# Channel normalisations by image pairs, three of them moved into the first deformable convolution

## The chip, the cores and the metric

The kernel runs on one core of one Trainium2 chip. The metric is the device time of one launch in microseconds (us); the median of three runs is 826.81 us (823.98 to 828.96).

## The reference

The input x is 8 images of 64 channels by 16 x 16 pixels, in float32. Four blocks follow, each with a residual add and each on a normalised copy of x (over the channels of every pixel):

```python
x = x + dcn_bn_relu(ln_c(x))          # 27-channel offset convolution, 9 sampled taps, batch norm, relu
t = tokens(x); t = t + lstm(ln_t(t))  # 256 steps, batch 8, hidden size 64
x = from_tokens(t); x = x + dcn(ln_c(x))
t = tokens(x); t = t + moe(ln_t(t))   # 8 experts, the best 2 of each token
# ln: (v - mean) / sqrt(var + eps)
```

## The kernel before

Partitions hold 128 channels: images 0 to 3 in the lower 64 and 4 to 7 in the upper 64, and the free axis holds four image pairs of 256 pixels, so `xs` is 128 x 1024. Each engine has its own program in program order, and semaphores join them: a wait stops everything behind it on its engine. The engines are TensorE (PE), VectorE (DVE), ScalarE (ACT) and GpSimd (POOL); SyncE (SP) issues the loads, small ones first (L340 to L355), then the expert weights.

A normalisation (`norm`, L395, L798 and L1216) goes over all 1024 columns at once: PE multiplies `xs` by a matrix of 1/64 for the means (L401), in two matmuls of 512 columns, each of two passes in float32; DVE subtracts (L1220), ACT squares (L804), PE makes variances with the squares as weights (L406, 16 passes of 2 columns), ACT takes the root (L806), DVE the reciprocal and a copy of each scale over 64 columns (L1225, L1227), PE turns them back by 8 transposes (L413), DVE multiplies (L1234). The first norm runs at the start; in its file stand also the maxima of the two sets of sampling weights (`largest`, L1333), their powers of two and the batch-norm column `bnw` (L1377 to L1387). ACT begins the convolution only when `bnw` is whole (L953). The second norm runs behind the first convolution, waits for all four residual adds (`c0_res`, L641), and takes in the recurrence's biases (`biases`, L602) while scales are made; then come the gates of row 0 (L599) and 256 recurrent steps (L658), in which PE, ACT and DVE hand over to one another and the rest of the work is laid into the gaps.

The first convolution (`conv(0)`) takes 8 images m, each in 9 steps g. On PE a step has the offsets of image m + 2 (L434, at g = 0 and 1; turned at g = 3, L443), `taps` (L456), `turn_weights(m, g)` (L469), which turns four blocks of the sampling weights `st`, and `sums` (L486), four steps behind. ACT's `high` (L870) and DVE's `low` (L1292) split each turned block into two float16 parts; `turn_weights` may be three blocks ahead of `low`, and `sums` waits for `low` too. ACT makes the tents of image m + 2 at g = 8 (L850, L854), and DVE their weighting (`weighted`, L1280), behind `low(m, 8)`. From these POOL makes `st` in six products of 768 columns for each image (`outer(m, t)`, L1143, three for each half t). After a pair is done (`turn`, L499, at g = 6 of the next even m, and ACT's `result`, L891) POOL adds it to `xs` (`add`, L1150). POOL's order is this, and the change leaves it as it is:

```python
for m, t in sorted(itertools.product(range(B), range(2)), key=lambda a: products(l, *a)):
    outer(m, t)
    if m % 2 == 0 and m > 3 and t == 0:
        add((m - 4) // 2)
for i in range(BQ - 2, BQ):
    add(i)
```

So pair 0 is added behind outer(4, 0), pair 1 behind outer(6, 0), and pairs 2 and 3 behind the last product.

## Time and profile before

| | us |
|---|---|
| median of three runs | 826.81 (823.98 to 828.96) |
| the profiled execution | 822.92 |
| its span, first to last instruction | 821.2 |
| PE busy in the span | 653.5 (80%) |
| DVE, ACT, POOL busy | 505.7, 421.4, 235.4 |

The span holds the start and first convolution (to about 136 us), the recurrence (from 146.5, at 1.58 us a step), the second convolution and the experts. Rows give the start and the busy time in us, the engine, the line, the operation, what it writes and reads with its shape, and a count where instructions of one kind are merged. In brackets stands how long the engine stood idle before, and what ended that. PE's matmuls are pipelined and their ends modelled. PEclk is TensorE's granted clock, 1.00 for 2.4 GHz.

### The profile page before, as it was taken

The page shows a single profiled execution, that of the slowest core. Times are in us where ns is not written, and L with a number is a line of the kernel's source. Part 1 is how long each engine was busy: PE and PEld are TensorE (multiplying, and loading weights), DVE is VectorE, ACT ScalarE, POOL GpSimd, SP SyncE. Part 2 cuts the span into 40 slices and gives each one's busy share as a digit, 9 for nine tenths or more (in the row PEclk, how much of TensorE's full clock was granted, in tenths as well). Part 3 has the DMA queues.
Part 4 walks back from the last instruction along what each step waited for, and adds up shares of the span by engine and source line. Part 5 has one row for each costly group of instructions (what it writes and reads, how often), then busy time and mean ns, then how long its engine had stood idle before and what let it go on. Part 6 is the DMA issues. An engine that isn't in the chain of part 4 may idle for free.

```text
span 821.2 us, 16043 instructions
## 1 busy us (share of the span) xinstructions
PE 653.5 (80%) x5315; PEld 524.9 (64%) x5315; DVE 505.7 (62%) x1672; ACT 421.4 (51%) x1492; POOL 235.4 (29%) x209
## 2 busy tenths in 40 slices
PE   5799998666787667776689888976899961999991
PEld 3478787555566555655566656654788961788881
DVE  4688884456654566655434444344888878688883
ACT  3476775233333555553334444446677771677760
POOL 0587682000000000000002100000887601677751
PEclk9999999555555555555555555555899985899996
DMA  9910000000000000000000000000000000111112
GB/s 211 212 32 2 2 2 1 2 1 0 1 2 1 1 1 1 2 0 1 1 0 2 1 1 2 1 1 1 1 2 2 2 2 29 23 28 27 28 21 81
DMA packets 12769, 14.97 MB, mean 18 GB/s; under 512 B 5873, under 2 KB 8626, under 8 KB 12690
## 3 DMA queue, kind: packets, MB, share of 16 engines
q1 hardware_dynamic: 9906, 11.26, 6.1%
q0 software_dynamic: 2496, 2.56, 1.5%
q8 instruction: 45, 0.74, 0.4%
q14 instruction: 34, 0.28, 0.1%
q10 hardware_dynamic: 288, 0.13, 0.1%
HBM read 11.62 MB, written 2.33 MB: 17 GB/s over the span
## 4 chain that ended last, share of the span: by engine, by line
PE 58%; DVE 17%; ACT 13%; issue 8%; DMA 2%; DVEq 1%; SPq 1%; POOL 0%; POOLq 0%; ACTq 0%
PE bank L486 7%; DVE bank L1510 6%; PE duo L736 6%; PE duo L664 6%; PE bank L664 5%; DVE hr L1514 4%; PE bank L469 4%; ACT duo L1036 4%; PE duo L434 4%; ACT bank L1040 4%; PE duo L666 3%; PE bank L666 3%; PE bank L747 3%; PE bank L762 3%; PE duo L469 3%
## 5 line engine op out<-in xcount | busy, mean ns | idle before, releaser
L1143 POOL TENSOR_TENSOR st<-tent,tentx 128x768 f32<-128x768 f32 x72 | 112.5, 1592 | 172.9 <-DVE tentx L1284 123.5
L1510 DVE TENSOR_TENSOR_SCAN bank<-duo,scan_add 64x24 f32<-64x24 f32 x256 | 52.8, 206 | 125.4 <-ACT duo L1036 125.1
L1143 POOL TENSOR_TENSOR st<-sq 128x768 f32<-128x768 f32 x9 | 13.2, 1500 | 305.7 <-DVE sq L1499 305.7
L668 PE MATMUL bank<-hr,lv 64*64 64x8 f32 x512 | 91.5, 251 | 0.0
L664 PE MATMUL bank<-hr,lv 64*64 64x8 f32 x256 | 48.5, 261 | 51.5 <-DVE hr L1514 51.4
L664 PEld LDWEIGHTS bank<-hr,lv 64*64 64x64 f32 x256 | 36.3, 201 | 81.2 <-DVE hr L1514 81.1
L664 PE MATMUL duo<-hr,lv 64*64 64x8 f32 x256 | 48.5, 261 | 46.5 <-DVE hr L1514 46.2
L664 PEld LDWEIGHTS duo<-hr,lv 64*64 64x64 f32 x256 | 36.3, 201 | 76.3 <-DVE hr L1514 76.0
L1514 DVE SCALAR_TENSOR_TENSOR hr<-tog,bank 64x8 f32<-64x8 f32 x256 | 39.6, 155 | 73.4 <-ACT bank L1040 73.4
L668 PEld LDWEIGHTS bank<-hr,lv 64*64 64x64 f32 x512 | 84.4, 223 | 0.0
L486 PE MATMUL bank<-zw,shi 128*128 128x128 f16 x576 | 79.6, 220 | 1.1 <-ACT osb L880 0.8
L486 PE MATMUL bank<-zw,hid 128*128 128x128 f16 x576 | 79.6, 220 | 0.0
L1292 DVE SCALAR_TENSOR_TENSOR hid<-bank,shi 128x512 f16<-128x512 f32 x96 | 64.7, 686 | 18.5 <-ACT shi L870 17.9
L1036 ACT ACTIVATE duo<-duo 64x16 f32<-64x16 f32 x128 | 19.6, 153 | 102.1 <-PE duo L666 101.9
L870 ACT ACTIVATE shi<-bank 128x512 f16<-128x512 f32 x96 | 57.2, 596 | 28.2 <-PE bank L469 27.3
L1036 ACT ACTIVATE duo<-bank 64x16 f32<-64x16 f32 x128 | 19.6, 153 | 93.6 <-PE bank L666 93.4
L469 PE MATMUL bank<-ident,st 128*128 128x128 f32 x384 | 60.5, 282 | 1.6 <-DVE hid L1292 1.4
L486 PEld LDWEIGHTS bank<-zw,shi 128*128 128x128 f16 x576 | 56.7, 99 | 2.2 <-DVE hid L1292 1.9
L486 PEld LDWEIGHTS bank<-zw,hid 128*128 128x128 f16 x576 | 56.7, 98 | 1.6
L736 PE MATMUL duo<-w13s,st 128*128 x312 | 54.1, 318 | 1.3 <-ACT st L1087 1.3
L1040 ACT ACTIVATE bank<-bank 64x8 f32<-64x8 f32 x256 | 37.6, 147 | 29.7 <-DVE bank L1510 2.2
L1038 ACT ACTIVATE tog<-bank 64x8 f32<-64x8 f32 x256 | 43.8, 171 | 15.2
(257 smaller groups left out, 1564.4 us busy)
## 6 DMA issues: line engine op xcount, KB each, us to landing
w13s<-w SPq DMA_DIRECT2D x16, 320.0 KB
w2s<-w SPq DMA_DIRECT2D x4, 320.0 KB
st<-yrows SPq DMA_DIRECT2D x2, 512.0 KB, 4.6
st<-xrows,xidx POOLq DMA_INDIRECT x39, 2.5
yrows<-st,yidx POOLq DMA_INDIRECT x39, 2.2
samw<-sample_w SPq DMA_DIRECT2D x2, 288.0 KB, 4.2
xs<-x SPq DMA_DIRECT2D x2, 256.0 KB, 4.2
xrows<-st SPq DMA_DIRECT2D x1, 512.0 KB, 2.6
```

Of the source, the lines that this page charges most:

```text
L469: mm = nc.tensor.transpose(bank[3 + g % RING][:, k * 128:k * 128 + 128], st[m % 2][:, t, tap, half * 128:half * 128 + 128], ident[:, :])
L486: mm = nc.tensor.matmul(bank[6][:, lo:lo + 2 * C], part[:, place(p, h), k, :], zw[p][:, half, tap, :, :].rearrange("p k c -> p (k c)"), st ...
L664: nc.tensor.matmul(both[:, 0, t, :], lv[:, C:2 * C], prev, start=False, stop=True, skip_group_check=True)
L668: nc.tensor.matmul(go, lv[:, 2 * C:3 * C], prev, start=False, stop=True, skip_group_check=True).then_inc(s("l_o"), 1)
L736: mm = nc.tensor.matmul(duo[m][:, half * 512:half * 512 + n], xts[:, t % 3, :], w16[:, bass.ds(e * SLOT + at, n)], start=(part == 0), stop ...
L870: nc.scalar.activation(shi[:, place(m % 2, g), :, :].rearrange("p k n -> p (k n)"), bank[3 + g % RING][:, :], ACT.Copy, scale=SSCALE / (1 ...
L1036: nc.scalar.activation(gate_in[:, 1:3, :], both, ACT.Tanh).then_inc(s("l_act"), 1)
L1040: nc.scalar.activation(tcell[:, :], cell[:, :, 2], ACT.Tanh, scale=0.5).then_inc(s("l_tc"), 1)
L1143: nc.gpsimd.tensor_tensor(st[p][:, t, k:k + KG, :].rearrange("p k (y x) -> p k y x", x=16), ty, tx, ALU.mult)\
L1292: nc.vector.scalar_tensor_tensor(out=slo[:, place(m % 2, g), :, :].rearrange("p k n -> p (k n)"), in0=bank[3 + g % RING][:, :], scalar=SSC ...
L1510: nc.vector.tensor_tensor_scan(cell[:, :, :].rearrange("p b k -> p (b k)"), gates, scan_add[:, :, :].rearrange("p b k -> p (b k)"), 0.0, A ...
L1514: nc.vector.scalar_tensor_tensor(out=hr[:, n % (2 * W), :], in0=tog[:, :], scalar=1.0, in1=tcell[:, :], op0=ALU.add, op1=ALU.mult).then_in ...
```

## The change

- SP loads the second set of sampling weights (`samw[1]`) fifth, and the second offset weights (`convw[1]`) later, under another semaphore.
- Both normalisations go by pairs of 256 columns, with helpers on each engine. At the start pair 0 is done through to its scaled columns first, and the roots, scales and scaling of the other three come inside the convolution's first images. ACT's wait for `bnw` stands behind `pads(2)`.
- Of the second normalisation, pair i = 0, 1, 2 is centred, squared and its variance taken inside the convolution, at m = 3, 5 and 7: PE's mean at g = 1 (behind a wait for that pair's add), DVE's centring at g = 2, ACT's square at g = 3, PE's variance at g = 5, and DVE's copy of it into `dev` at g = 6. Mean and variance lie in free or finished columns of bank 7. Pair 3 is done behind the convolution, and one root takes the three kept pairs.
- The scales of the recurrence's input are turned and applied in two halves of the rows: the first half ahead of step 0 (row 0 first), the second in steps 0 to 3.

```diff
             sp.dma_start(convb[:, :], conv_b).then_inc(s("ld_conv"), 16)
             sp.dma_start(samw[0][:, :], sample_w[0]).then_inc(s("ld_conv"), 16)
             sp.dma_start(bnp[:, :], bn).then_inc(s("ld_conv"), 16)
+            sp.dma_start(samw[1][:, :], sample_w[1]).then_inc(s("ld_conv"), 16)
             sp.dma_start(rank_c[:, :], consts[:, 2 * P:2 * P + E]).then_inc(s("ld_const"), 16)
             sp.dma_start(tent_c[:, :, :, :, :].rearrange("p a b c d -> p (a b c d)"),
                          consts[:, 2 * P + E:]).then_inc(s("ld_const"), 16)
-            sp.dma_start(convw[1][:, :, :, :], conv_w[1]).then_inc(s("ld_conv"), 16)
-            sp.dma_start(samw[1][:, :], sample_w[1]).then_inc(s("ld_late"), 16)
+            sp.dma_start(convw[1][:, :, :, :], conv_w[1]).then_inc(s("ld_late"), 16)
...
-            def norm(l, ready, middle=None, end=None):
...
+            def mean_of(i, to):
+
+                nc.tensor.matmul(to, mean_w[:, :], pixels(xs, 0, P, i), start=True, stop=True)\
+                    .then_inc(s("n_mean"), 1)
+
+            def variance_of(l, i, to, start):
+
+                pe.wait_ge(s("n_sq"), BQ * l + i + 1)
                 for j in range(2):
+                    mm = nc.tensor.matmul(to[:, 2 * j:2 * j + 2], sq[:, i * T + j * 128:i * T + j * 128 + 128],
+                                          mean_w[:, 0:P:C], start=(start and j == 0), stop=True,
+                                          skip_group_check=True)
+                return mm
...
+            def turn_scales(i):
+
+                for j in range(2):
+                    mm = nc.tensor.transpose(bank[(0, 5, 6, 7)[i]][:, T + j * 128:T + j * 128 + 128],
+                                             sq[:, i * T + j * 128:i * T + j * 128 + 128], ident[:, :])
+                mm.then_inc(s("n_rt"), 1)
+
+            def turn_row_scales(q):
+
+                pe.wait_ge(s("n_rb"), 3 + q)
+                for i in range(BQ):
+                    mm = nc.tensor.transpose(bank[2 - q][:, i * 128:i * 128 + 128],
+                                             sq[:, i * T + q * 128:i * T + q * 128 + 128], ident[:, :])
+                mm.then_inc(s("n_rt"), 1)
 
...
+                        if l == 0:
+                            pe.wait_ge(s("n_keep"), i)
...
                 offsets(0, 0)
                 offsets(0, 1)
+                if l == 0:
+                    pe.wait_ge(s("n_rb"), 2)
+                    turn_scales(1)
                 turn_offsets(0)
                 pe.wait_ge(s(c + "taps"), 2)
                 taps(0, 0)
+                if l == 0:
+                    turn_scales(2)
+                    turn_scales(3)
                 offsets(1, 0)
                 offsets(1, 1)
                 turn_offsets(1)
                 taps(0, 1)
+                if l == 0:
+                    pe.wait_ge(s("n_xn"), BQ)
                 for m in range(B):
                     for g in range(NG):
+                        if l == 0 and m > 2 and m % 2 == 1:
+                            if g == 1:
+                                pe.wait_ge(s("c0_res"), m // 2)
+                                mean_of(m // 2 - 1, bank[7][:, T:2 * T])
+                            elif g == 5:
+                                variance_of(1, m // 2 - 1, bank[7][:, 0:4], True).then_inc(s("n_var"), 1)
                         if m + 2 < B:
                             if g < 2:
                                 offsets(m + 2, g)
...
-            norm(0, [("ld_x", 32)], turn_max, spread)
+            pe.wait_ge(s("ld_x"), 32)
+            mean_of(0, bank[0][:, 0:T])
+            mean_of(1, bank[5][:, 0:T])
+            variance_of(0, 0, bank[4][:, 0:4], True).then_inc(s("n_var"), 1)
+            mean_of(2, bank[6][:, 0:T])
+            mean_of(3, bank[7][:, 0:T])
+            pe.wait_ge(s("n_rb"), 1)
+            turn_scales(0)
+            variance_of(0, 1, bank[4][:, 4:8], False)
+            variance_of(0, 2, bank[4][:, 8:12], False)
+            turn_max()
+            variance_of(0, 3, bank[4][:, 12:16], False).then_inc(s("n_var"), 1)
+            spread()
             pe.wait_ge(s("ld_conv"), 16 * 5)
-            pe.wait_ge(s("n_xn"), 2)
             conv(0)
...
-            norm(1, [("c0_res", BQ)], biases)
-            pe.wait_ge(s("n_xn"), 4)
+            pe.wait_ge(s("c0_res"), BQ)
+            mean_of(3, bank[1][:, 0:T])
+            variance_of(1, 3, bank[2][:, 0:4], True).then_inc(s("n_var"), 1)
+            biases()
+            turn_row_scales(0)
+            pe.wait_ge(s("n_xn"), 5)
...
-                if n == POWER + 2:
+                if n == 1:
+                    turn_row_scales(1)
+                    pe.wait_ge(s("n_xn"), 6)
+                elif n == POWER + 2:
...
+                    if n == 7 * W + SLOTS[0]:
+                        pe.wait_ge(s("n_xn"), 8)
                     gates_x(r + 1, SLOTS.index(t))
...
+            def square_of(l, i):
+
+                act.wait_ge(s("n_xc"), BQ * l + i + 1)
+                nc.scalar.activation(pixels(sq, 0, P, i), pixels(xc, 0, P, i), ACT.Square).then_inc(s("n_sq"), 1)
+
+            def root_of(src, lo, hi, eps):
+
+                nc.scalar.activation(dev[:, lo:hi], src, ACT.Sqrt, bias=epsc[:, eps:eps + 1]).then_inc(s("n_sd"), 1)
...
+                    if l == 0:
+                        act.wait_ge(s("n_xn"), b4 + 1)
...
+                if l == 0:
+                    act.wait_ge(s("n_var"), 2)
+                    root_of(bank[4][:, 4:16], 4, 16, 0)
+                    act.wait_ge(s("ld_conv"), 16 * 5)
+                    nc.scalar.activation(bnw[:, 0:1], bnp[:, 3:4], ACT.Sqrt, bias=epsc[:, 1:2]).then_inc(s("bn_a"), 1)
+                    nc.scalar.preload_act_table(ACT.Sigmoid)
                 offsets(0)
...
+                if l == 0:
+                    act.wait_ge(s("bn_d"), 6)
+                    act.wait_ge(s("c_scale"), 2)
...
+                        if l == 0 and m > 2 and m % 2 == 1 and g == 3:
+                            square_of(1, m // 2 - 1)
...
-            norm(0, 0, ACT.Sqrt)
-            act.wait_ge(s("ld_conv"), 16 * 5)
-            nc.scalar.activation(bnw[:, 0:1], bnp[:, 3:4], ACT.Sqrt, bias=epsc[:, 1:2]).then_inc(s("bn_a"), 1)
-            nc.scalar.preload_act_table(ACT.Sigmoid)
-            act.wait_ge(s("bn_d"), 6)
-            act.wait_ge(s("c_scale"), 2)
+            nc.scalar.preload_act_table(ACT.Sqrt)
+            square_of(0, 0)
+            square_of(0, 1)
+            act.wait_ge(s("n_var"), 1)
+            root_of(bank[4][:, 0:4], 0, 4, 0)
+            square_of(0, 2)
+            square_of(0, 3)
             conv(0)
 
 
-            norm(1, 1, ACT.Tanh)
+            nc.scalar.preload_act_table(ACT.Sqrt)
+            act.wait_ge(s("n_keep"), 3)
+            root_of(dev[:, 0:12], 0, 12, 1)
+            square_of(1, 3)
+            act.wait_ge(s("n_var"), 6)
+            root_of(bank[2][:, 0:4], 12, 16, 1)
+            nc.scalar.preload_act_table(ACT.Tanh)
             def high_part(k):
...
+            def centre_of(l, i, src):
+
+                dve.wait_ge(s("n_mean"), BQ * l + i + 1)
+                nc.vector.tensor_tensor(pixels(xc, 0, P, i), pixels(xs, 0, P, i), src, ALU.subtract)\
+                    .then_inc(s("n_xc"), 1)
+
+            def scales_of(lo, hi):
+
+                dve.wait_ge(s("n_sd"), 1 if lo == 0 else 2)
+                nc.vector.reciprocal(dev[:, lo:hi], dev[:, lo:hi]).then_inc(s("n_rs"), 1)
+                dve.wait_ge(s("n_rs"), 1 if lo == 0 else 2)
+                nc.vector.tensor_copy(sq[:, lo * C:hi * C].rearrange("p (k c) -> p k c", c=C),
+                                      dev[:, lo:hi].unsqueeze(2).broadcast_to([P, hi - lo, C])).then_inc(s("n_rb"), 1)
+
+            def scaled(i):
+
+                dve.wait_ge(s("n_rt"), i + 1)
+                nc.vector.tensor_tensor(pixels(xn, 0, P, i), pixels(xc, 0, P, i), bank[(0, 5, 6, 7)[i]][:, T:2 * T],
+                                        ALU.mult).then_inc(s("n_xn"), 1)
+
+            def row_scales(q):
+
+                nc.vector.tensor_copy(half_rows(sq[:, :], q).rearrange("p b (k c) -> p b k c", c=C),
+                                      half_rows(dev[:, :], q).unsqueeze(3).broadcast_to([P, BQ, 2, C]))\
+                    .then_inc(s("n_rb"), 1)
+
+            def scaled_rows(q, lo, hi):
+
+                dve.wait_ge(s("n_rt"), BQ + q + 1)
+                nc.vector.tensor_tensor(half_rows(xn[:, :], q)[:, :, lo:hi], half_rows(xc[:, :], q)[:, :, lo:hi],
+                                        bank[2 - q].rearrange("p (b n) -> p b n", b=BQ)[:, :, lo:hi],
+                                        ALU.mult).then_inc(s("n_xn"), 1)
...
-                    dve.wait_ge(s("n_xn"), 2)
                     flats(0)
-                    split_taps(l)
+                    normalised()
...
                 distances(0)
+                if l == 0:
+                    scaled(1)
                 weighted(0)
                 tap_images(0, 0)
+                if l == 0:
+                    scaled(2)
+                    scaled(3)
                 distances(1)
                 flats(1)
...
+                        if l == 0 and m > 2 and m % 2 == 1:
+                            if g == 2:
+                                centre_of(1, m // 2 - 1, bank[7][:, T:2 * T])
+                            elif g == 6:
+                                i = m // 2 - 1
+                                dve.wait_ge(s("n_var"), 3 + i)
+                                nc.vector.tensor_copy(dev[:, 4 * i:4 * i + 4], bank[7][:, 0:4])\
+                                    .then_inc(s("n_keep"), 1)
                         if g == 3 and m + 2 < B:
...
-            def largest():
+            def largest(l):
 
                 dve.wait_ge(s("ld_conv"), 80)
-                dve.wait_ge(s("ld_late"), 32)
-                for l in range(2):
-                    nc.vector.tensor_reduce(cmax[:, l:l + 1], samw[l][:, :], AX.X,
-                                            ALU.max, apply_absolute_value=True).then_inc(s("c_max"), 1)
+                nc.vector.tensor_reduce(cmax[:, l:l + 1], samw[l][:, :], AX.X,
+                                        ALU.max, apply_absolute_value=True).then_inc(s("c_max"), 1)
 
...
+            def normalised():
+
+                scales_of(4, 16)
+                split_taps(0)
+                dve.wait_ge(s("bn_a"), 1)
+                nc.vector.reciprocal(bnw[:, 1:2], bnw[:, 0:1]).then_inc(s("bn_d"), 1)
...
+            centre_of(0, 0, bank[0][:, 0:T])
+            centre_of(0, 1, bank[5][:, 0:T])
+            scales_of(0, 4)
+            centre_of(0, 2, bank[6][:, 0:T])
+            largest(0)
+            centre_of(0, 3, bank[7][:, 0:T])
+            scaled(0)
+            largest(1)
+            power("c", cpow, bank[3], KTOP)
+            dve.wait_ge(s("c_bc"), 1)
+            nc.vector.reciprocal(csc[:, :, 0], bank[3][:, 256:258]).then_inc(s("c_scale"), 1)
+            nc.vector.tensor_scalar(csc[:, :, 1], bank[3][:, 256:258], 2.0 ** (KTOP - ZTOP) / SSCALE, None,
+                                    ALU.mult).then_inc(s("c_scale"), 1)
             conv(0)
-            norm(1)
-            dve.wait_ge(s("n_xn"), 3)
+            centre_of(1, 3, bank[1][:, 0:T])
             nc.vector.memset(gates, 0.0).then_inc(s("l_zero"), 1)
+            dve.wait_ge(s("n_sd"), 4)
+            nc.vector.reciprocal(dev[:, :], dev[:, :]).then_inc(s("n_rs"), 1)
+            dve.wait_ge(s("n_rs"), 3)
+            row_scales(0)
+            scaled_rows(0, 0, W)
+            scaled_rows(0, W, 128)
 
...
+                if n == 0:
+                    row_scales(1)
+                elif 2 <= n <= 3:
+                    scaled_rows(1, 64 * (n - 2), 64 * (n - 1))
```

## Rows read from the trace of the kernel before

**Rows 1.** Table of stretches, the convolution; us, busy us (instructions) by engine, PEclk, DMA

```profile
core 0: us, PE busy (x) PEld busy (x) DVE busy (x) ACT busy (x) POOL busy (x), PEclk, DMA share, GB/s
40.00:130.00 90.00, 87.73 (x948) 73.27 (x947) 77.22 (x118) 64.31 (x143) 66.38 (x45) 1.00 0.05 12
```

**Rows 2.** Timeline of the start, all engines

```profile
6.19 3.75 PE L401 MATMUL duo<-xs,mean_w 128*128 128x512 f32 x4 [6.19 <-DMA xs<-x]
...
9.74 3.51 PE L406 MATMUL duo<-mean_w,sq 128*128 128x2 f32 x16
...
12.60 1.41 DVE L1338 TENSOR_REDUCE cmax<-samw 128x1 f32<-128x576 f32 x2 [1.92 <-DMA rw<-router]
...
16.85 0.58 PE L561 MATMUL duo<-cpow,ones 1*128 1x2 f32 x2
...
18.61 1.70 ACT L823 COPY pad<-xn 64x256 f32<-64x256 f32 x4 [2.13 <-DVE bnw L1387]
...
19.59 5.25 PE L434 MATMUL duo<-pad,convw 128*27 128x256 f32 x12 [2.16 <-ACT pad L823]
...
26.23 2.77 PE L434 MATMUL duo<-pad,convw 128*27 128x256 f32 x12
```

**Rows 3.** Chain that ended last, from the last add to the recurrence; start, us, what

```profile
135.55 0.73 POOL xs L1150
136.33 1.14 PE duo L401 x2
...
138.89 1.95 PE duo L406 x16
140.84 1.04 PE duo L594 x4
...
142.31 1.91 PE duo L413 x8
...
144.99 1.11 PE duo L599 x8
...
146.53 0.31 PE duo L664 x2
```

**Rows 4.** Timeline of PE, one recurrent step

```profile
149.68 0.38 PE L664 MATMUL duo<-hr,lv 64*64 64x8 f32 x2 [0.78 <-DVE hr L1514]
```

**Rows 5.** Timeline of ACT, a table load and the instruction behind it

```profile
13.58 1.28 ACT L808 ACT_TABLE_LOAD   x1
...
14.88 0.29 ACT L951 ACTIVATE bnw<-bnp,epsc 128x1 f32<-128x1 f32 x1
```

**Rows 6.** Timelines of DVE, POOL and PE in the convolution, around the adds

```profile
74.22 0.45 DVE L1280 TENSOR_TENSOR tentx<-tent,sig 128x288 f32<-128x288 f32 x1
...
74.84 4.63 POOL L1143 TENSOR_TENSOR st<-tent,tentx 128x768 f32<-128x768 f32 x3 [4.72 <-PE duo L469]
79.44 0.72 POOL L1150 TENSOR_TENSOR xs<-xs,ores 128x256 f32<-128x256 f32 x1
...
106.42 0.72 POOL L1150 TENSOR_TENSOR xs<-xs,ores 128x256 f32<-128x256 f32 x1
...
123.05 0.73 POOL L1150 TENSOR_TENSOR xs<-xs,ores 128x256 f32<-128x256 f32 x1
...
75.10 1.48 PE L434 MATMUL duo<-pad,convw 128*27 128x256 f32 x6
...
123.91 0.60 PE L469 MATMUL bank<-ident,st 128*128 128x128 f32 x4
```

**Rows 7.** Table of stretches and PE's timeline, where its clock moved; columns as in rows 1

```profile
133.00:136.00 3.00, 1.16 (x8) 0.97 (x8) 0.00 (x0) 1.72 (x4) 0.45 (x1) 1.00 0.00 0
...
670.00:671.00 1.00, 0.26 (x3) 0.16 (x2) 0.93 (x3) 0.01 (x1) 0.00 (x0) 1.00 0.00 0
...
673.00:674.00 1.00, 0.00 (x0) 0.00 (x0) 0.90 (x5) 0.99 (x3) 0.00 (x0) 0.60 0.00 0
...
567.58 2.73 PE L434 MATMUL duo<-pad,convw 128*27 128x128 f32 x12 [2.08 <-ACT pad L823]
...
570.00:571.00 1.00, 0.55 (x4) 0.20 (x3) 0.00 (x0) 0.36 (x1) 0.00 (x0) 0.60 0.00 0
```

More of the change, by code:

```diff
@@ L262, in build, with half_rows @@
             s(n)
-        def nth(l):
-            return min(l, 2)
+        def half_rows(t, q):
+            return t.rearrange("p (b q n) -> p b q n", b=BQ, q=2)[:, :, q, :]
         def pixels(t, p0, p1, b4):
@@ L394, in _ @@
         def _(pe):
-            def norm(l, ready, middle=None, end=None):
-                for wait_sem, v in ready:
-                    pe.wait_ge(s(wait_sem), v)
-                for j in range(2):
-                    nc.tensor.matmul(bank[j][:, :], mean_w[:, :], xs[:, j * 512:j * 512 + 512],
-                                     start=True, stop=True).then_inc(s("n_mean"), 1)
-                for j in range(8):
-                    if j % 4 == 0:
-                        pe.wait_ge(s("n_sq"), 2 * nth(l) + j // 4 + 1)
-                    mm = nc.tensor.matmul(bank[2][:, 2 * j:2 * j + 2], sq[:, j * 128:j * 128 + 128],
-                                          mean_w[:, 0:P:C], start=(j == 0), stop=True, skip_group_check=True)
-                mm.then_inc(s("n_var"), 1)
-                if middle:
-                    middle()
-                pe.wait_ge(s("n_rb"), nth(l) + 1)
-                for j in range(8):
-                    mm = nc.tensor.transpose(bank[j // 4][:, j % 4 * 128:j % 4 * 128 + 128],
-                                             sq[:, j * 128:j * 128 + 128], ident[:, :])
-                    if j % 4 == 3:
-                        mm.then_inc(s("n_rt"), 1)
-                if end:
-                    end()
```

71 lines of the change are left out of this document (17 added, 54 removed).

## The prediction

> **What bounds the kernel now.** I read the table of stretches first, then the timeline and the chain of waits at three places: the start, the seam between first convolution and recurrence, and the third and fourth image of the convolution. In the convolution [rows 1] the reader is to see that TensorE (PE) is busy 87.73 of 90 us, with VectorE at 77.22, ScalarE at 64.31 and GpSimd (POOL) at 66.38: time added to PE there, or a wait of PE, is paid almost in full, since the other engines catch up while it stands. The unused rest, 2.27 us of 90, is some 0.3 us for an image of about 13 us. Ahead of it stands a serial start [rows 2]: x lands, the first mean matmul goes at 6.19, and the first offset convolution only at 19.59. Behind it stands a serial seam [rows 3]: the last add on POOL at 135.55, the whole normalisation after it, the recurrence's first matmul at 146.53. The change works on both seams and puts the difference into the PE-bound part.
>
> **Start.** Before, DVE waits for the last small load before it takes the two maxima (12.60, 1.41 us), and ScalarE's pads wait for the batch-norm column until 18.61 [rows 2]. Afterwards the first pair's pads wait for its own scaled columns alone, and what ends last is PE's queue. Its order, at the pace of those rows: two means of 256 columns, half of the 3.75 us of L401, so ready at 7.4 and 8.3; DVE's centring and ScalarE's square of pair 0 to 8.35; its variance, a quarter of the 3.51 us of L406, to about 9.3; two means, 1.75, to 11.05; two transposes, a quarter of the 1.91 us of the seam's L413 [rows 3], to 11.55; two variances to 13.4; the maxima's transposes, taken at the 0.58 us of L561, to 14.0; the fourth variance to 14.95; the spread matmul, 0.58, to 15.55. So the offsets start near 15.6 instead of 19.59: 4.0 us early. samw1 is now fifth in the queue and convw1 goes behind; the first is needed at 12.3 and was complete at 12.60 even as a late load, so nothing waits for either. Of the rest, turn_scales(1) hides behind ScalarE's bias copy of the offsets, the other two pairs' transposes (4, at full pace about 0.5 us) come ahead of the second image's offsets on PE, and DVE's three scalings fall into idle time ahead of the next distances. Net: **-3.5**. Bounds: -2 if PE takes a second longer to come to full pace, which it did while the 12 passes of 19.59 ran (5.25 us, against 2.77 at 26.23), -5 if that happens sooner.
>
> **Seam.** Only pair 3 is left there. From 136.33 [rows 3]: the mean of 256 columns instead of 512, about 0.7 instead of 1.14; centring and square, 1.42 us from the end of the mean to 138.89, go to about 0.95; 4 variance passes instead of 16, 0.5 instead of 1.95; the biases, 1.47 us between 140.84 and 142.31, stay and hide root, reciprocal and the copy of half the scales; four transposes instead of eight, 0.96 instead of 1.91; one scaling of 64 columns, about 0.3 instead of the 0.77 between 144.22 and 144.99; the gates' 1.54 stay. That ends at 142.75: **-3.8**, between -3 (half pace already at the mean) and -4.5. The other row half costs its four transposes behind the step n = 1: 0.96 us against 0.78 us of PE idle in a step [rows 4], **+0.2**, at most +1; DVE's copies and scalings of n = 0 to 3 stand in steps whose weight maxima start only at n = 4, and hide.
> A table load is where a rule can be weighed: ScalarE's next instruction starts at 14.88, 0.02 us after a load of 1.28 us from 13.58 [rows 5]. So the square-root table, loaded while POOL adds, is there in time, and the sum above holds. The Trainium skill (ScalarE: Activation LUTs, What ACT_TABLE_LOAD costs) adds a drain and gives about 2.66 us for a switch; by that the square of pair 3 would wait some 0.6 us and the seam bring -3.2 as an estimate from that page. The trace disagrees with it by the 0.02 us.
>
> **Inside the convolution, work.** At m = 3, 5 and 7 PE gets a mean (2 passes of 256 columns, 0.23 each by the 2.77 us for 12 at 26.23 [rows 2]) and a variance (4 passes at 0.12 by 138.89 [rows 3]): 0.96 us, three times **+2.9**. DVE gets a centring of 256 columns and a copy of 4, ScalarE a square, some 1.4 us together at each place. They stand in one file (low g = 2, centring, square, high g = 3), so they delay DVE's chain by about 0.95 us; PE itself is later by more than that at that point, so I take nothing, and keep 0 to +1 for each of m = 3 and 5.
>
> **Inside the convolution, the new wait.** This is the step that decides. PE takes mean_of(0) at m = 3, g = 1, behind a wait for c0_res 1, and that is POOL's add(0). POOL's order is not changed: add(0) stands behind outer(4, 0), which needs weighted(4), and DVE makes that at m = 2, g = 8. The rows [rows 6] show the three in a line: DVE's tentx at 74.22, POOL's three products from 74.84, the add at 79.44 for 0.72, so xs is ready at 80.16. PE is at that place (ahead of offsets(5, 1)) at 75.10. It would stand 80.2 - 75.1 = 5.1 us. Queued behind it on PE are the second half of the offsets, all turn_weights of the image and the sums, so ScalarE's highs and DVE's lows run dry as well; nothing else feeds PE. The same pattern comes once more, at m = 5 (the add at 106.42 [rows 6]). At m = 7 the add is at 123.05 and done at 123.77, PE is there at 123.91: no wait. Nothing in the change brings the add forward, since start and image 2 shift all engines alike. Two waits, less the 0.3 us of slack each: **+9.6**. Bounds: +8 (POOL at its best pace and more slack found), +11 (m = 7 late as well).
> **The clock after such a gap.** PE fell idle in 670 to 671, and within 673 to 674, whose mean is 0.60, its granted clock fell from 1.00 to 0.50, the 1.2 GHz level: some 3 us after the last matmul [rows 7]. A gap of 5.1 us is longer than that, so I expect the fall at both places. After dense work began at 567.58 the clock rose within 570 to 571, 3 us later [rows 7]; at the start it took 5.25 us at half pace [rows 2]. Of 3 to 5.3 us at half pace half is lost: 1.5 to 2.6, I take 2.1, twice **+4.2**; without a fall 0.
> The Trainium skill (TensorE: Matmul & The Clock Gate, Why this matters for your kernels) warns of idle gaps between matmul bursts as what throws the clock back to its half rate. By that rule each of the two waits costs more than its own length; the trace agrees, in the fall at 673.
>
> **Sum.** -3.5 - 3.8 + 0.2 + 2.9 + 9.6 + 4.2 = **+9.6 us**. The profiled execution took 822.92 us, its span and 1.7 us around it; with the sum, 832.5. The median of the runs shown is 826.81, 3.9 above it, and the sum does not hang on that difference: 826.81 + 9.6 = **836.4 us**, 1.2% slower. About 0.5% (4.1 us) is what a measurement of this kernel can tell from no change.
>
> **The rivals.** (a) The clock holds through the gaps. For it: PE had only 1.16 us of matmul between 133 and 136 and the granted clock stayed at 1.00 [rows 7]. Against: that was broken by bursts, this gap is not. Then +5.4: 832.2, slower by 0.65%. (b) The wait costs nothing, faster. Its mechanism is that add(0) is done before PE gets to g = 1 of m = 3, because PE is held back in image 2 or POOL gets weighted(4) earlier. It decides if the add ends 5.1 us earlier against PE. Price: no waits, no clock loss, -4.2: 822.6, 0.5% faster. Against it stands the row itself: the products before the add alone take 4.6 us, and they start with the data of the last step of the image before. (c) The waits come, but their gap is filled: DVE and ScalarE are ahead when PE resumes and some of the 2.27 us idle and the start's early clock bring more than I gave; start -5, seam -4.5, the step +0.2, work +2.9, waits +8, no fall: +1.6, 828.4, no difference. (d) Dearer: DVE's chain adds 1 us at m = 3 and 5 and the clock takes 5.3 us to return: 9.6 + 2 + 1.1 = +12.7, 839.5.
>
> **How the numbers follow.** My forecast with its bounds, 0.58; (d) 0.08; (a) 0.18; (c) 0.08; (b) 0.08. The likeliest is the forecast. The range 830.5 to 840.5 holds it with its bounds taken one at a time, (d) and most of (a), about 0.8, and leaves out (b) and (c). Slower by over 0.5%: 0.58 + 0.08 + 0.18 less 0.04 for the low end of (a), 0.80; within 0.5%: that 0.04, (c), and some 0.02 of (b), 0.14; faster 0.06.
>
> **What would show it.** In the changed profile: the first L434 row near 15.6; the recurrence's first matmul some 6.5 us after the end of the last add, where it was 10.2; PE idle before mean_of(0) and mean_of(1) for about 5 us each, released by POOL's xs, and none before mean_of(2); PE's granted clock at 0.50 for 3 to 5 us behind both. The prediction is wrong if PE has no such two gaps, or if the first offsets and the recurrence do not move.

## The result and the profile after

The changed kernel takes 840.34 us (median of six runs, 838.25 to 841.30), the kernel before 827.67 beside it (823.98 to 828.96): ratio 1.0169, 95% interval 1.0143 to 1.0194, slower. The direction was right. The ratio is just past the high end of the range (840.5 / 826.81 = 1.0166); the two medians differ by 12.7 us, where 9.6 was forecast, and 840.34 itself lies just inside, so the interval covers the end of the range. The profiled execution took 838.25 us with a span of 836.5, where before it was 822.92 and 821.2: 15.3 us more in the two spans, 12.7 in the medians.

First PE's waits from 20 to 165 us, longest first; the columns are the total in us, the times, and the longest one.

```profile
PE bank L397 <- POOL xs L1205: 10.0, 2, 5.0
PE duo L438 <- issue: 4.0, 1, 4.0
```

The first line is new, and it is the predicted wait: PE's mean (L397) stands twice for 5.0 us until POOL has added the pair (L1205). The timelines of POOL and PE at both places, and then at the third mean, show the three in a file:

```profile
78.45 0.72 POOL L1205 TENSOR_TENSOR xs<-xs,ores 128x256 f32<-128x256 f32 x1
...
79.22 1.22 PE L397 MATMUL bank<-xs,mean_w 128*128 128x256 f32 x2 [5.02 <-POOL xs L1205]
...
113.46 0.72 POOL L1205 TENSOR_TENSOR xs<-xs,ores 128x256 f32<-128x256 f32 x1
...
114.23 1.22 PE L397 MATMUL bank<-xs,mean_w 128*128 128x256 f32 x2 [5.02 <-POOL xs L1205]
...
138.95 0.65 PE L397 MATMUL bank<-xs,mean_w 128*128 128x256 f32 x2
```

The third mean, at 138.95, has no such bracket. Next, the table of stretches (columns as in [rows 1]) around the first of these gaps and behind the second:

```profile
75.00:77.80 2.80, 0.00 (x0) 0.00 (x0) 2.08 (x3) 0.00 (x0) 2.80 (x3) 0.97 0.00 0
77.80:84.60 6.80, 5.38 (x19) 2.83 (x20) 0.00 (x0) 0.39 (x1) 5.71 (x5) 0.51 0.00 0
84.60:111.00 26.40, 24.32 (x259) 20.02 (x255) 20.04 (x36) 18.95 (x44) 11.62 (x8) 1.00 0.01 2
111.90:118.80 6.90, 4.57 (x12) 2.07 (x13) 0.25 (x1) 0.00 (x0) 6.62 (x5) 0.51 0.00 0
```

PE does nothing from 75.0 to 77.8, and in the next 6.8 us its granted clock is at half, the 1.2 GHz level: that is why the mean takes 1.22 us. The convolution before never left 1.00 [rows 1].

The start, from its timeline (all engines):

```profile
15.66 4.72 PE L438 MATMUL duo<-pad,convw 128*27 128x256 f32 x12
...
24.52 12.64 POOL L1198 TENSOR_TENSOR st<-tent,tentx 128x768 f32<-128x768 f32 x8 [22.92 <-DVE tentx L1349]
...
26.11 1.96 DVE L1339 TENSOR_TENSOR dist<-tent_c,omt 128x576 f32<-128x576 f32 x1 [0.36 <-ACT omt L876]
...
29.50 0.82 ACT L862 COPY pad<-xn 64x256 f32<-64x256 f32 x2
...
30.41 2.73 PE L438 MATMUL duo<-pad,convw 128*27 128x256 f32 x6 [3.99 <-issue]
```

The same place in the kernel before (VectorE's distances of the second image, PE's offsets of the third):

```profile
30.13 0.88 DVE L1270 TENSOR_TENSOR dist<-tent_c,omt 128x576 f32<-128x576 f32 x1 [0.65 <-ACT omt L837]
...
33.32 1.48 PE L434 MATMUL duo<-pad,convw 128*27 128x256 f32 x6 [2.86 <-ACT pad L823]
```

The offsets start at 15.66 for 19.59 [rows 2], as predicted. The third image's offsets do not keep that: PE stands 3.99 us before them, for 2.86, and runs them at half pace (2.73 us; 1.48 before).

And the seam, from the chain that ended last (start, us, what), to be held against [rows 3]:

```profile
151.69 0.73 POOL xs L1205
152.42 0.04 issue
152.46 0.98 PE duo L397 x2
...
154.39 1.02 PE duo L404 x4
155.41 1.04 PE duo L625 x4
...
156.87 1.06 PE duo L420 x4
...
158.23 1.11 PE duo L630 x8
...
159.77 0.31 PE duo L699 x2
```

From the end of the last add to the first recurrent matmul it is 7.35 us, where it was 10.25 [rows 3].

With these lines the whole difference can be laid out. The table gives, for each profiled execution, the start of VectorE's first low part (L1292 before, L1361 after), the time from the first low part of image m to that of the next, image 7 to its last low part, from the start of the last add to the last multiply of step 0 (L1514, L1607), the 255 further steps, and what is left of the span. The missing columns, m = 2, 4, 6 and the way from the last low part to the last add, are 13.85, 13.85, 9.47 and 4.14 us everywhere (in e10 to e12 m = 4 is 14.24).

```
                 first   m=0    m=1    m=3    m=5   m=7   seam   steps    rest
before           36.05  12.98  12.51  13.14  12.45  7.11  12.34  413.11  260.2
after            34.56  12.61  13.41  21.16  20.43  8.22   9.45  415.37  260.0
e1_add_first     34.35  13.70  13.41  13.90  13.58  8.21   8.79  415.38  262.6
e2_waits_only    37.65  12.31  12.46  19.93  19.85  7.11  13.74  413.03  260.0
e3_filled        35.07  12.32  13.40  18.71  18.38  8.25   8.93  415.40  262.5
e4_start_only    34.50  12.58  13.41  13.14  12.45  7.11  13.75  413.52  261.3
e5_pads_early    32.87  13.49  12.46  13.90  13.57  8.22   9.70  415.32  262.7
e8_before_shift5 36.81  13.19  13.40  13.14  12.45  7.11  12.32  412.71  261.5
e9_start_pads    32.23  13.27  12.46  13.14  12.45  7.11  12.33  413.01  261.6
e10_late         34.01  13.69  13.41  13.14  13.00  8.22   9.70  415.22  262.7
e12              32.38  13.49  12.46  13.14  12.99  8.22   9.39  412.17  260.1
```

After less before: -1.5, -0.4, +0.9, **+8.0, +8.0**, +1.1, -2.9, +2.3, -0.2, in all +15.3.

Each row is one execution, and some columns move with the moment at which the granted clock falls. The old seam took 12.3 us where the clock fell 5 to 6 us behind the start of the last add (before, e8, e9), and 13.75 where it fell 0.3 and 1.2 us behind it (e2, e4), with the same code.

### The profile page after: what moved, and what is told of

Its sections match the earlier page's. It is cut to its first block, busy times and chain, and to the rows that moved or that the text cites. A ratio compares the mean times of both kernels' runs of the same rounds, so it can differ in the third digit from the quotient of the medians.

```text
span 836.5 us, 16090 instructions
## 1 busy us (share of the span) xinstructions
PE 659.6 (79%) x5323; PEld 529.0 (63%) x5323; DVE 504.1 (60%) x1686; ACT 420.8 (50%) x1497; POOL 234.3 (28%) x209
## 4 chain that ended last, share of the span: by engine, by line
PE 57%; DVE 16%; ACT 13%; issue 10%; DMA 2%; POOL 1%; DVEq 1%; SPq 0%; POOLq 0%; ACTq 0%
PE bank L490 6%; PE duo L776 6%; DVE bank L1603 6%; PE duo L699 6%; PE bank L699 5%; DVE hr L1607 4%; PE bank L473 4%; ACT duo L1091 4%; ACT bank L1095 4%; PE duo L438 4%; PE duo L701 3%; PE bank L701 3%; PE bank L787 3%; PE bank L802 3%; PE duo L473 2%
## 5 line engine op out<-in xcount | busy, mean ns | idle before, releaser
L1361 DVE SCALAR_TENSOR_TENSOR hid<-bank,shi 128x512 f16<-128x512 f32 x96 | 65.0, 686 | 34.6 <-ACT shi L909 33.7
L1607 DVE SCALAR_TENSOR_TENSOR hr<-tog,bank 64x8 f32<-64x8 f32 x256 | 39.7, 155 | 74.6 <-ACT bank L1095 74.6
```

The costliest lines, as they stand in the source:

```text
L1361: nc.vector.scalar_tensor_tensor(out=slo[:, place(m % 2, g), :, :].rearrange("p k n -> p (k n)"), in0=bank[3 + g % RING][:, :], scalar=SSC ...
L1607: nc.vector.scalar_tensor_tensor(out=hr[:, n % (2 * W), :], in0=tog[:, :], scalar=1.0, in1=tcell[:, :], op0=ALU.add, op1=ALU.mult).then_in ...
```

## The experiments

The theory was that the two waits, with the half clock behind them, make the slowdown. The rivals: the added work in the PE-bound convolution; a start or seam that failed; and, for the recurrence's +2.3, something in the program's layout.

**e1: the add goes first.** GpSimd is idle before the product that the add stood behind.

```diff
+                    if l == 0 and m % 2 == 0 and m > 3 and t == 0:
+                        add((m - 4) // 2)
                     outer(m, t)
-                    if m % 2 == 0 and m > 3 and t == 0:
+                    if l == 1 and m % 2 == 0 and m > 3 and t == 0:
                         add((m - 4) // 2)
```

> The changed kernel, but GpSimd runs the add of image pairs 0 and 1 ahead of the product of the even image that it stood behind (in the first convolution only). ores of pair 0 is ready at 70.3 us and GpSimd is idle from 68.9 to 73.9, so the add ends near 71.1, before TensorE comes to the mean at 74.2. Theory (the two waits on the add and the half clock behind them make the slowdown): both 5.0 us gaps of TensorE go, and no half clock near 78 and 112; step m=3 and step m=5 fall back from 15.1 and 16.5 us to about 13.2 and 14.6 (12.1 and 13.5 before, and 1.1 of added work, as step m=7 shows). That is 4 us less in all than the waits and the clock: 14 less 0.2, so 838.25 - 13.8 = 824.5 for the profiled execution and 840.3 - 13.8 = 826.5 for the median, against 827.7 before: ratio 0.996 to 1.001. Rival (the added instructions on TensorE, VectorE and ScalarE, and the stir they make in the convolution, cost the time, and the wait only shows where it is lost): at most half of it goes, 833 or more, ratio over 1.006.

Measured: 825.73 us (twelve runs) against 825.36, ratio 0.9999 (0.9981 to 1.0016). The timelines of POOL and PE:

```profile
71.23 0.73 POOL L1205 TENSOR_TENSOR xs<-xs,ores 128x256 f32<-128x256 f32 x1 [1.45 <-ACT ores L930]
...
74.92 0.65 PE L397 MATMUL bank<-xs,mean_w 128*128 128x256 f32 x2
```

The add is done 3 us before PE asks, nothing stands, and the granted clock is 1.00 from 75 to 120. Moving one line takes back the whole 1.7%. Steps m = 3 and 5 keep 0.8 and 1.1 us over the kernel before: that is the work.

**e2: the waits alone**, in the kernel before.

```diff
                     for g in range(NG):
+                        if l == 0 and m in (3, 5) and g == 1:
+                            pe.wait_ge(s("c0_res"), m // 2)
```

> The kernel before, with nothing but two waits added: TensorE waits for the add of pair 0 at m=3, g=1 and for that of pair 1 at m=5, g=1; no work is added or moved. Theory: TensorE is the bound there, so each wait costs its whole length (it comes at 75.1 and 102.2 where the adds end at 80.2 and 107.2 or later, 5 us each) and the half clock behind it 2 us more: 827.7 + 14 = 841.7, ratio 1.017, TensorE idle 5 us at L434 before each and a granted clock of 0.50 for some 7 us from about 3.5 us into each gap. Rival (other engines' slack takes the waits up, and the added work is what costs): 828 to 832, ratio under 1.006.

Measured: 839.11 us, ratio 1.0163 (1.0135 to 1.0191). PE's waits from 60 to 120 us, and the stretches behind the two gaps:

```profile
PE duo L434 <- POOL xs L1152: 10.0, 2, 5.0
```

```profile
79.70:86.50 6.80, 5.43 (x27) 3.52 (x28) 0.69 (x1) 1.00 (x3) 5.65 (x5) 0.53 0.01 2
...
113.80:120.60 6.80, 5.75 (x30) 3.77 (x30) 0.69 (x1) 1.14 (x3) 5.33 (x5) 0.53 0.00 0
```

Two waits with no work behind them cost what the whole change costs (6.8 and 7.4 us in the table). With e1 it settles the cause from both sides. The trace also bears on the start, whose code is that of the kernel before:

```profile
33.17 2.76 PE L434 MATMUL duo<-pad,convw 128*27 128x256 f32 x6 [2.86 <-ACT pad L825]
...
31.50:38.30 6.80, 5.13 (x14) 2.19 (x15) 4.75 (x7) 2.16 (x5) 6.80 (x5) 0.50 1.10 207
```

Behind the same gap of 2.86 us, after which PE ran at full pace in the kernel before, the granted clock is at half here; in e8 it also fell, at 34.2.

**e3: the gap filled.** Ten matmuls, whose results are overwritten, ahead of each of the two waits (and behind a wait for their output columns to be free), in the changed kernel.

```diff
                             if g == 1:
+                                pe.wait_ge(s("c0_out_sb"), m // 2)
+                                for _ in range(10 if m < 7 else 0):
+                                    nc.tensor.matmul(bank[7][:, T:2 * T], mean_w[:, :], pixels(xs, 0, P, 3),
+                                                     start=True, stop=True)
                                 pe.wait_ge(s("c0_res"), m // 2)
```

> The changed kernel, and ahead of the two waits TensorE multiplies ten times the mean matrix by 256 columns of pair 3 into the half bank that the mean takes next (about 0.49 us each, 4.9 us: what the wait lasts), so that it stands still no longer; the results are overwritten. Theory of the clock: the wait ends when it did, but no half clock follows at 78 and 112, the mean takes 0.49 us again for 1.22, the offsets behind it 1.41 for 2.69, steps m=3 and m=5 13.1 for 15.1 and 14.5 for 16.5: 838.25 - 4 = 834.2 for the profiled execution, 836.3 for the median. Rival (the half clock costs nothing, since other engines have slack enough, or the dummy work delays the rest): 840 or more.

Measured: 835.48 us, ratio 1.0118 (1.0092 to 1.0144). PE's timeline at m = 3, and the stretch around it:

```profile
74.26 4.54 PE L544 MATMUL bank<-xs,mean_w 128*128 128x256 f32 x20
79.46 0.70 PE L397 MATMUL bank<-xs,mean_w 128*128 128x256 f32 x2 [0.67 <-POOL xs L1209]
80.09 1.48 PE L438 MATMUL duo<-pad,convw 128*27 128x256 f32 x6
```

```profile
75.00:90.00 15.00, 14.34 (x132) 12.01 (x131) 8.27 (x15) 6.64 (x16) 8.76 (x7) 1.00 0.00 0
```

The wait ends when it did, the clock stays at 1.00, and the offsets take 1.48 us again. So each 8.0 us divides: for m = 3 (m = 5) the half clock is 21.16 - 18.71 = 2.45 (2.05), the wait 18.71 - 13.90 = 4.81 (4.80), the work 13.90 - 13.14 = 0.76 (1.13).

**e4: the start alone.** The second normalisation goes back whole behind the convolution (the code of the kernel before, with the changed semaphore counts).

> The changed kernel's start alone: the first normalisation by image pairs; all four pairs of the second behind the convolution, as before. Theory: the start's gain is real but TensorE's longer gap before the third image's offsets (4.0 us for 2.9) and the half clock behind it take most of it: step m=3 is reached 0.9 us earlier than before and the seam lasts 10.2 us: 822.9 - 0.9 = 822.0 for the profiled execution, 826.8 for the median, ratio 0.998 to 1.000. Rival (the start gives its full 3.5 us, lost later by what was put into the convolution): 824.2, ratio 0.996. Second rival (the 2 us that the changed kernel lost inside the recurrence come from the program's new layout at the start): 828.8.

Measured: 824.28 us against 825.36, ratio 0.9986 (0.9970 to 1.0002). The 2 us in the recurrence do not come with the start (413.52). By the traces the start brings 1.0 us over the kernel before: 1.5 at the first low part and 0.4 in m = 0, less 0.9 in m = 1. The median alone does not exclude the full 3.5 us: in e4's trace the old seam took 1.4 us more than in the kernel before, which hides part of a gain.

**e5: what ate the start's gain.** On top of e1, ScalarE pads the third image ahead of the second's tents, in the time in which it waits for VectorE's distances anyway.

```diff
                 taps(0, 1)
+                if l == 0:
+                    pads(2)
                 tents(1)
-                pads(2)
+                if l == 1:
+                    pads(2)
```

> e1_add_first, and ScalarE copies the third image's padded input (pads(2)) ahead of the tents of the second image instead of behind them, in the first convolution. ScalarE is idle from 26.96 to 28.10 there, waiting for VectorE's distances, and the copies take 0.82, so nothing else moves. Theory (the start's gain is lost because TensorE stands 4.0 us before the third image's offsets, where it stood 2.9, and the clock falls behind that): the gap falls to 1.0 to 1.6 us, no half clock between 29 and 36, the first low part comes 2 to 3 us earlier than in e1_add_first and the step from the first to the second image takes 12.3 to 12.6 us for 13.7: 2.5 to 4 us less than e1_add_first, ratio to before 0.995 to 0.997. Rival (GpSimd's products of images 0 and 1, 9.5 us each from 24.5 on, or VectorE's time beside them, set the pace there): under 1.2 us less, ratio 0.998 to 1.001.

Measured: 820.79 us against 825.27, ratio 0.9942 (0.9923 to 0.9961), more than expected. The timeline:

```profile
26.18 1.96 DVE L1344 TENSOR_TENSOR dist<-tent_c,omt 128x576 f32<-128x576 f32 x1 [0.35 <-ACT omt L876]
...
26.92 0.83 ACT L862 COPY pad<-xn 64x256 f32<-64x256 f32 x2
27.85 1.46 PE L438 MATMUL duo<-pad,convw 128*27 128x256 f32 x6 [1.34 <-issue]
```

PE's gap falls from 3.99 to 1.34 us, the offsets run at full pace, the first low part comes at 32.87 and m = 1 takes 12.46. A half clock still comes, later (from 37.3 to 40.8, behind a gap of 2.13 us), within m = 0, which takes 13.49. (The profiled execution took 825.28 us, 4.5 more than the median, so its table row understates the gain.)

**e6 and e8: the recurrence's 2 us.** In the kernel before, four of the 255 steps take 1.93 us for 1.58 with nothing in the way, in the changed kernel eight others. Step 22 of the kernel before on VectorE, and the ScalarE row that it waits for:

```profile
181.10 0.15 DVE L1514 SCALAR_TENSOR_TENSOR hr<-tog,bank 64x8 f32<-64x8 f32 x1 [0.28 <-ACT bank L1040]
...
182.19 0.21 DVE L1510 TENSOR_TENSOR_SCAN bank<-duo,scan_add 64x24 f32<-64x24 f32 x1 [0.43 <-ACT duo L1036]
183.03 0.15 DVE L1514 SCALAR_TENSOR_TENSOR hr<-tog,bank 64x8 f32<-64x8 f32 x1 [0.64 <-ACT bank L1040]
...
182.43 0.15 ACT L1040 ACTIVATE bank<-bank 64x8 f32<-64x8 f32 x1
```

ScalarE is done at 182.58; the multiply starts 0.45 us later, 0.1 in a usual step. Both experiments move VectorE's later instructions by a few places (three in e6, on top of e1; five in e8, in the kernel before):

```diff
+            for k in range(3):
+                nc.vector.memset(csc[:, 0, k % 2:k % 2 + 1] if k < 2 else csc[:, 1, k % 2:k % 2 + 1] if k < 4 else cmax[:, 0:1], 0.0)
             nc.vector.memset(ones[:, :], 1.0).then_inc(s("l_init"), 1)
```

> e1_add_first, and three more memsets of one column at the very start of VectorE's program, where it waits for xs until 6.7 us; nothing else. It tests where the changed kernel's 2 us inside the recurrence come from: steps of 1.93 us for 1.58 in which VectorE starts the last multiply of the step 0.35 us late with everything it waits for done. Counted in VectorE's instructions, these multiplies stand at places 62 of 64 (19, 38, 114, 133, 153 by 64, and two later places), in the kernels before, after and of the start alone. Theory (VectorE stands 0.35 us at every 64th instruction of its program, and the change has moved the step's last multiply onto such places more often): three instructions more move all of 19, 38, 114, 133, 153, 175 and 196 off, one (142) comes on; the 255 steps take 413.2 us for 415.4, 2.1 us less than e1_add_first. Rival (the steps are slow by time or by what runs beside them): the same steps stay slow, 415.4.

Measured: 414.03 us for the steps (1.35 less; 2.1 expected), median 824.11, ratio 0.9977 (0.9956 to 0.9998). All seven named steps became quick; 142 did not become slow, and 76, 95, 195 and 216 did.

> The kernel before, with five one-column memsets at the start of VectorE's program and nothing else. By the same count no last multiply of a step stands at place 62 of 64 any more: the steps 22, 79, 136 and 199 (1.93 us) go back to 1.58 and 145 (2.16) to 1.8 or less; the 255 steps take 411.3 to 411.8 us for 413.1, the median 1.3 to 1.8 us less, ratio 0.998 to 0.9985. Rival (the slow steps don't hang on VectorE's place in its program): 413.1, the same steps slow, ratio 1.000.

Measured: 412.71 us for the steps (0.40 less), median 825.72, ratio 0.9998 (0.9979 to 1.0017): no gain in the median. All four named steps became quick, 145 stayed, 177 became slow. So the slow steps do hang on the place in VectorE's program, and the rival falls; but the count by 64 missed some. Laid over six traces, a count by 128 fits without exception: a step's last multiply at place 62 or 64 of 128 is late, at 59 to 61, 63 and 65 to 67 it is not (step 2 is slow by the second row half, put into step 1; why 200 is slow is not known). The count takes in the waits of VectorE's program; over the trace's own records, from 0, the places are 63 and 65. Both are one place: where the multiply stands at 64, it is the scan of its step, two places ahead, that is late. Step 175 of the changed kernel shows it, a scan 0.46 us behind the end of the ScalarE row that it waits for (442.16):

```profile
442.62 0.21 DVE L1603 TENSOR_TENSOR_SCAN bank<-duo,scan_add 64x24 f32<-64x24 f32 x1 [0.60 <-ACT duo L1091]
```

In all 14 traces, each of the 51 multiplies and 20 scans at place 62 started about 0.35 us later behind its wait than is usual, and no multiply at another place did. e12 puts the count to the test.

**e7: e5 and e6 together.**

> e5_pads_early and e6_shift3 together. Theory: the two add up, 4.5 to 6 us less than e1_add_first, ratio to before 0.992 to 0.995. Rival: the pace elsewhere takes them up, 0.996 or more.

Measured: 821.85 us, ratio 0.9955 (0.9935 to 0.9974), 3.9 us under e1 and not under e5. The steps took 414.05 us, as in e6; the medians do not add up (e5 gained 4.9 us on e1, e6 1.6), which their intervals of 1.6 us to either side allow, and the expectation of 4.5 to 6 was too high.

**e9: is the part inside the convolution worth anything?** e4 with the early pads of e5.

> e4_start_only with the pads of the third image early as in e5: the whole second normalisation stays behind the convolution. It asks whether the part inside the convolution is worth anything once its waits are gone. Theory (a wash: 0.8 + 1.1 + 1.1 us of added TensorE time per pair, against some 3.5 us less at the seam and 2 us more of slow steps in the recurrence): 819.5 to 821.5, within 0.2% of e5's 820.8, ratio to before 0.992 to 0.996. Rival (the seam's part is worth its 3.5 us): 823 to 825, ratio 0.997 to 0.999.

Measured: 821.12 us, ratio 0.9943 (0.9922 to 0.9965), the same as e5. By the traces the part inside the convolution gains 2.6 us at the seam (9.70 for 12.33), and pays 3.0 in m = 3, 5 and 7 and 2.3 in the steps; the medians, 820.79 and 821.12, show no difference.

**e10: PE asks later.** GpSimd's order stays; for pairs 0 and 1 the mean moves from g = 1 to g = 6, and the centring, square and variance behind it move as well (not shown).

```diff
-                        if l == 0 and m > 2 and m % 2 == 1:
-                            if g == 1:
+                        if l == 0 and (m, g) in ((3, 6), (5, 6), (7, 1)):
```

> The changed kernel with GpSimd's order left as it is, and TensorE's mean of pairs 0 and 1 moved from g=1 to g=6 of images 3 and 5, the steps behind it with it (centre at g=7, square at g=8, the variance and the copy of it at g=1 and g=2 of the next image); pair 2 stays. TensorE comes to the mean near 82 and 110 us, the adds end at 79.2 and 107. Theory (what costs is where TensorE waits, not the work): no wait on the add in images 3 and 5, no half clock there, the same as e1_add_first, 825 to 827, ratio to before 0.998 to 1.002. Rival (the add's place behind GpSimd's product hurts in itself, as ores then comes free late for the next pair): 830 or more.

Measured: 824.28 us against 826.45, ratio 0.9972 (0.9956 to 0.9989). POOL's and PE's timelines:

```profile
79.01 0.72 POOL L1205 TENSOR_TENSOR xs<-xs,ores 128x256 f32<-128x256 f32 x1
...
81.44 0.65 PE L397 MATMUL bank<-xs,mean_w 128*128 128x256 f32 x2
```

The add's place does not hurt in itself. The work costs less here, too: 0.0, 0.4 and 0.55 us in m = 3, 4 and 5, for 0.76 and 1.13 in e1.

**e11 and e12: everything together.** e11 is e10 with the early pads; e12 adds four memsets on VectorE, the number for which no step's multiply stands at place 62 or 64 of 128.

> e10_late and the early pads of e5 together: the whole change with both repairs. Theory: the two don't touch, so 824.3 less the 3 to 4.5 us that the early pads gave in e5 and e9: 820 to 821.5, ratio to before 0.991 to 0.995, no better than e5 and e9 beyond 0.2%. Rival (the late mean spares the work inside the convolution too, since step m=3 of e10 lasted 13.14 us as before): 817 to 819, ratio 0.988 to 0.991.

Measured: 821.93 us, ratio 0.9946 (0.9926 to 0.9965): the ratio as the theory had it, the time 0.4 us above its 820 to 821.5.

> e11_late_pads and four one-column memsets at the start of VectorE's program. The runs so far corrected the count of e6 and e8: in the traces of before, after, e4, e6, e8 and e10 every recurrent step whose last multiply stands at place 62 or 64 of 128 of VectorE's program is 0.35 us late, and no other place near it (steps 2 and 200, slow for another reason, aside). That explains the misses of e6 (142 stayed quick, 76 and 95 came) and e8 (145 stayed, 177 came). With four more instructions no step's multiply stands at such a place. Theory: the eight slow steps of e11 (19, 38, 114, 133, 153, 175, 196, 237) all go and none comes, the 255 steps take 412.3 us for 415.1; the median falls by 2.8 us to 819.1, ratio to before 0.990 to 0.993. Rival (the places were fitted to the runs by chance): three to eight slow steps stand somewhere, 413.4 or more.

Measured: none of the eight slow steps is left and none has come; the 255 steps take 412.17 us (412.3 expected). The median is 818.63 us (six runs) against 825.05, ratio 0.9929 (0.9904 to 0.9954). This version is faster than both kernels, by 0.7% than the one before: the whole change, with the means of two pairs moved, one copy moved and four empty instructions. e9 with such a shift was not run, so it is not shown that the part inside the convolution adds to that.

## Why the prediction was right and wrong

- **The waits: right, to 0.1 us.** +9.6 was the term, 4.81 + 4.80 was measured; the third mean had no wait. Rival (b), the add done before PE asks, fell at the row it was argued from, and e1 shows what it would have been worth.
- **The clock behind them: right.** +4.2 predicted, 2.45 + 2.05 measured, with a fall 3.5 and 2.6 us into the gaps. The half clock lasted 6.8 us, longer than the 3 to 5 I gave, but part of it lay over the rest of the gap, where PE had nothing to run. Rival (a) fell.
- **The work: right.** +2.9 predicted, 0.76 + 1.13 + 1.11 = 3.0 measured. In e10 it cost 0.0 + 0.4 + 0.55 + 1.1, a third less, so the place matters as well.
- **The start: the step that failed most.** -3.5 was the term, -1.0 the measurement. The first 4 us came as worked out. But the step took the gain at the first offsets for that of the whole start ("start and image 2 shift all engines alike"), and that was wrong: GpSimd's first product came 4.4 us earlier and VectorE's distances of the second image 4.0, and beside each other these distances now took 1.96 us for 0.88. ScalarE's pads stand behind them, so PE's gap before the third image grew from 2.86 to 3.99 us: 1.1 of the 4 us. Another 1.3 went as the clock fell behind that gap (offsets of 2.73 us for 1.48). That the growth of the gap brought the fall is not shown: behind the old gap of 2.86 us the clock fell in e2 and e8 as well, and held in the one profiled execution of the kernel before. Up to the end of m = 1 the changed kernel is 1.0 us ahead of that execution, 1.8 ahead of e2 and 2.8 ahead of e8, so part of this miss is luck, in the clock and in how VectorE and GpSimd fall together. I had priced the start by its first offsets and not by the next thing that PE waits for. e5 cut the gap to 1.34 us and gained 4.9 us on e1.
- **The seam: mechanism right, term too large.** -3.8 was the term, -2.9 the measurement. The clock fell 1.1 us behind the start of the last add, at 152.8, before 5.2 us behind it, at 140.7, so mean and variance ran at half pace (0.98 and 1.02 us in the chain, for 0.7 and 0.5 in the sum), which is 0.8 of the missing 0.9; -3 was the bound for that case. Where it fell 3.0 us behind the add (e1) the seam took 8.79 us, -3.55; at 1.1 us (after) 9.45, at 0.5 us (e5, e10) 9.70. The step that failed here took the clock's fall from where the old seam had it, and that moves too: against the old seam with an early fall (13.75 us, e4) the new one gains 4.3.
- **The recurrence: not foreseen.** +0.2 was the term, for step 1, and +2.3 the measurement. Step 1 to 2 does cost 0.2. Of the other 2.1 us, 1.4 are slow steps that new instructions on VectorE, far ahead of them, moved onto bad places (e6, e8, e12): eight of 0.35 us for four. Step 200 is another 0.3; the rest is not accounted for.
- In all, the terms that decided the sign (waits, clock, work) were right to 0.5 us. What failed are the net of the start (2.5 us too large), the seam (0.9) and the recurrence (2.1 us put at nothing): 5.5 of the 5.7 us between the forecast and the two spans. That rival (d) came to the 12.7 us of the medians is luck; its terms, a longer VectorE chain and a longer half clock, are not what was measured. What stays open: the last part of the span took 260.0 to 264.1 us from one profiled execution to another, in kernels that differ little there. The traces place 2.6 us of it at the start of the second convolution: from the recurrence's last multiply to the seventh low part, 24.9 us in the kernel before, where the granted clock first rose 9.8 us behind that multiply, and 27.5 in e1, where it stayed at half for 26 us. Why it rose so differently is not known, and it is one reason why sums of one trace and medians differ by a few us. Nor was the new order of the loads tried by itself.

## What to carry to other kernels

Before a wait is put on the engine that bounds a stage, compare two rows: when the engine gets there, and when the awaited instruction ends, with all that is queued ahead of it on its own engine. If the second is later, here nearly every microsecond was paid, and almost half as much again as the clock fell; the cure is often to move one line, on either side. A gain at the start of a pipeline is worth what the next wait of the bounding engine leaves of it, so follow it to the next gap.

## What the hardware showed that was not expected

- **VectorE stands about 0.35 us at one place in every 128 of its program**, and it shows where a dependent chain has no slack: a step of 1.58 us becomes 1.93. In 14 traces, all 71 multiplies and scans of the recurrence at that place were late, and the forecast of e12 rested on it. Four empty instructions were worth 3.0 us of the recurrence (415.13 to 412.17). The Trainium skill (Runtime: NRT & Kernel Launch, Instruction fetch mechanics) has instructions fetched in blocks of 256, mostly hidden; that these stalls are such a fetch is not shown here, and the period that the runs show is 128.
- **VectorE's distances took from 0.76 to 1.96 us**: 0.76 at 25.98 in the kernel before, with GpSimd idle, up to 1.96 beside GpSimd's products of 1.58 each on average, by how the two fall together. With the five memsets of e8 m = 1 took 13.40 us for 12.51, and its distances 1.58 for 1.37; no work had changed there. The Trainium skill (SBUF — State Buffer, Who interferes with whom) says that a VectorE instruction with two SBUF inputs contends with a GpSimd one that reads SBUF, and that the port pair which they share is an exclusive lock; the rows agree, as the excess is never over one product.
- **The clock can fall within a dense convolution**: in the two gaps of 5.0 us the granted clock went from 1.00 to 0.50 before the gap ended and stayed there for 6.8 us, in the changed kernel and in e2 alike. The length of a gap alone did not tell whether it would: behind 2.86 us at the start it fell in e2 and e8 and held in the kernel before. In e5 it held through a gap of 1.34 us and fell behind the next one, of 2.13.
